# Counting graph edges on TensorE: ten chunks per PSUM bank, window offsets in registers, layer-norm sums by ScalarE

## The reference, cut to what matters

```python
x: (1250, 512) float32          # 1250 nodes
src, dst: (41250,) int32        # edges, both directions and one loop per node, sorted by dst
h = layernorm(x)                # mean and variance of each row of 512
for l in range(3):              # graph convolution
    h = relu(segment_sum((h @ W[l])[src] * norm, dst) + b[l])      # norm from the in-degrees
x = x + h                       # then: a small feed-forward part, a second graph layer,
                                # and a mixture of 16 experts with a shared one
```

## Time and profile before

| | us |
|---|---|
| median of 3 timed runs | 893.25 |
| lowest, highest | 893.14, 895.17 |
| the profiled execution's own time | 889.73 |
| its span in the profile | 887.7 |

### The profile page before, as it was taken

One profiled execution on the slowest core, in us unless ns is written; L12 is line 12 of the kernel. 1 busy time (PEld: TensorE's weight loads), 2 busy tenths in 40 slices (PEclk: granted clock), 3 DMA queues, 4 the chain that ended last, 5 costly groups with the idle time before them and its releaser, 6 DMA issues.

```text
span 887.7 us, 13725 instructions
## 1 busy us (share of the span) xinstructions
PE 807.3 (91%) x4032; PEld 624.7 (70%) x4033; DVE 554.3 (62%) x996; ACT 331.0 (37%) x624; POOL 141.9 (16%) x186
## 2 busy tenths in 40 slices
PE   4988799999999996998899987998989999999983
PEld 2444578888888875666788875787767777777761
DVE  7987491341242189789313479589557787778761
ACT  2567251341251111444221222332335556555541
POOL 2000000000000030000000330111313444455422
PEclk9999989999999998899999996996989999999997
DMA  7400000000000001000010302100989868965542
GB/s 189 136 1 1 2 1 0 1 1 1 1 1 1 6 25 49 1 1 1 0 48 1 113 1 66 50 1 1 327 287 365 223 170 288 326 195 82 127 92 35
DMA packets 32293, 71.39 MB, mean 80 GB/s; under 512 B 4387, under 2 KB 4637, under 8 KB 32243
## 3 DMA queue, kind: packets, MB, share of 16 engines
q1 hardware_dynamic: 24480, 53.31, 17.4%
q0 software_dynamic: 6272, 14.68, 8.3%
q10 hardware_dynamic: 1491, 2.73, 0.9%
HBM read 96.53 MB, written 12.72 MB: 123 GB/s over the span
## 4 chain that ended last, share of the span: by engine, by line
PE 72%; DVE 15%; issue 4%; ACT 3%; DMA 2%; ACTq 1%; DVEq 1%; POOL 0%; POOLq 0%
PE PS L1069 21%; PE PS L1103 9%; PE PS L1322 9%; PE PS L1369 8%; PE PS L1000 6%; PE PS L1201 5%; PE PS L1316 4%; PE PS L1144 3%; ACT CTR L717 2%; PE PS L1300 1%; DVE XN L1439 1%; PE PS L1331 1%; PE PS L1354 1%; PE PS L1043 1%; DVE stats L1846 1%
## 5 line engine op out<-in xcount | busy, mean ns | idle before, releaser
L1069 PE MATMUL PS<-CTR,YH 125*128 125x500 f32 (+1 forms) x480 | 164.1, 357 | 2.3 <-DVE YL L1620 2.3
L1069 PE MATMUL PS<-CTR,YL 125*128 125x500 f32 (+1 forms) x480 | 163.6, 356 | 0.0
L1069 PEld LDWEIGHTS PS<-CTR,YH 125*128 125x128 f32 x480 | 91.5, 191 | 15.6 <-DVE YL L1620 2.6
L1069 PEld LDWEIGHTS PS<-CTR,YL 125*128 125x128 f32 x480 | 91.6, 191 | 13.0
L1000 PE MATMUL PS<-ET 125*128 125x130 f16 x494 | 72.2, 303 | 16.0 <-ACT CTR L717 9.2
L1940 DVE TENSOR_TENSOR W1L<-WB,W1H 128x1152 fp32r<-128x1152 f32 x56 | 73.9, 1356 | 16.8 <-issue 8.4
L1369 PE MATMUL PS<-WB,YF 128*128 x168 | 76.9, 594 | 2.4 <-issue 1.7
L1647 DVE TENSOR_TENSOR ZL<-PS,ZH 128x500 fp32r<-128x500 f32 (+1 forms) x36 | 21.1, 591 | 90.1 <-ACT ZH L775 90.0
L1000 PEld LDWEIGHTS PS<-ET 125*128 125x128 f16 x494 | 39.9, 122 | 49.1 <-ACT CTR L717 28.7
L1322 PE MATMUL PS<-W1H,XGH 128*128 128x384 f32 x168 | 73.5, 438 | 0.0
L948 ACT CAST W1H<-WB 128x1152 fp32r x56 | 64.2, 1151 | 16.4 <-issue 10.3
(11 more groups left out here) (376 smaller groups left out, 1628.0 us busy)
## 6 DMA issues: line engine op xcount, KB each, us to landing
WB<-in_w SPq DMA_DIRECT2D x28, 1536.0 KB
WB<-in_w SPq DMA_DIRECT2D x28, 768.0 KB
WB<-in_b SPq DMA_DIRECT2D x28, 384.0 KB
X<-in_x SPq DMA_DIRECT2D x1, 2240.0 KB
xn_dram<-XN SPq DMA_DIRECT2D x1, 2240.0 KB
WNEXT<-in_W SPq DMA_DIRECT2D x2, 1024.0 KB, 9.5
SR<-in_sw SPq DMA_DIRECT2D x1, 1536.0 KB, 7.7
out<-X ACTq DMA_DIRECT2D x1, 1120.0 KB
```

The costliest lines, as they stand in the source:

```text
L1069: mm = nc.tensor.matmul(dest, lhs, rhs, start=(t == 0 and h == 0), stop=(t == NT - 1 and h == 1))
```

## The change

One PSUM bank now takes a whole batch (five pairs, ten chunks) with a window of 50 columns plus one (`BWIN`, 10 x 51 = 510 columns). A product has 12 columns for each of 10 tiles, and TensorE writes it at the pair's offset inside the bank's window. The offsets come from a table `off_i`, which VectorE computes once, and which TensorE reads into registers 25 at a time (five batches). Because the products only add, the bank is first set to zeros by a product of one row with a blank row of 510 columns (`open_bank`). It is issued for the next batch when the present one has two pairs left. `oh_next` is gone; one product of 10 columns for each batch (`first_column`) gives the last column of a window the edges that the next batch's first chunk still has for it, and it signals `group_done`, once a batch. ScalarE makes one copy of 10 x 50 columns for each batch.

Row sums of x (batches 2 to 11) and sums of squared deviations (batches 14 to 23) are taken by ScalarE with its accumulating output; VectorE then makes `XHAT` in ten operations after the last batch. The checks move into the batches (after batches 2 and 5), and TensorE waits for `counts_ready` only on the general way.

```diff
+PER = BATCH
+AHEAD_OF = 5
+CHECK_AT = 2
+FLAG_AT = 5
+SUMS_AT = 2
+SQUARES_AT = 14
+DEV_AT = 26
-WIN = 12
-SLOTS = WIN + 1
+SLOTS = 12
+BWIN = 50
+BKEYS = NT * (BWIN + 1)
+LAST_OFF = BWIN + 1 - SLOTS
...  ScalarE
+            for b in range(NBAT):
+                act.wait_ge(group_done, b + 1)
+                if b:
+                    act.wait_ge(placed, b)
+                nc.scalar.copy(CTR[0:NP, :, bass.ds(places[b % LOADS], BWIN)],
+                               PS[0:NP, b % 6, 0:BKEYS].rearrange("p (t w) -> p t w", t=NT)[:, :, 1:BWIN + 1]
                                ).then_inc(placed, 1)
+                t = b - SUMS_AT
+                if 0 <= t < NT:
...
+                    nc.scalar.activation(val[0:NP, t % 2, :], X[0:NP, t, :], ACT.Identity,
+                                         accum_out=sums[0:NP, 0, t:t + 1]).then_inc(sums_ready, 1)
+                t = b - SQUARES_AT
+                if 0 <= t < NT:
...
+                    nc.scalar.activation(val[0:NP, t % 2, :], X[0:NP, t, :], ACT.Square, bias=minus[0:NP, t:t + 1],
+                                         accum_out=sums[0:NP, 1, t:t + 1]).then_inc(sums_ready, 1)
...  TensorE
+            def first_column(b, past):
+                k = (b + 1) % RING
+                return nc.tensor.matmul(windows(b)[:, :, bass.ds(past, 1)], oh_lo[k][0:CHUNK, 0, :, 0],
+                                        oh_key[k][0:CHUNK, 0, :, 0].rearrange("p (t w) -> p t w", t=NT)[:, :, 0:1],
+                                        start=False, stop=True)
+
+            def open_bank(b):
+                if b >= 6:
+                    pe.wait_ge(placed, b - 5)
+                nc.tensor.matmul(PS[0:128, b % 6, 0:BKEYS], iota_lo[0:1, :, 0], blank[0:1, :], start=True, stop=False)
+
+            following = offsets(0)
+            open_bank(0)
+            for b in range(NBAT):
+                pe.wait_ge(onehot_ready, b + 1)
+                if b:
+                    first_column(b - 1, places[(b - 1) % AHEAD_OF * PER + PER - 1]).then_inc(group_done, 1)
+                if b % AHEAD_OF == 0:
+                    places = following
+                for j in range(PER):
+                    if j == PER - 2 and b + 1 < NBAT:
+                        open_bank(b + 1)
+                        if b % AHEAD_OF == AHEAD_OF - 1:
+                            following = offsets(b + 1)
+                    place = bass.ds(places[b % AHEAD_OF * PER + j - 1], SLOTS) if j else slice(0, SLOTS)
+                    for x in range(OWN):
+                        mm = nc.tensor.matmul(windows(b)[:, :, place], oh_lo[b % RING][0:CHUNK, j, :, x],
+                                              oh_key[b % RING][0:CHUNK, j, :, x].rearrange("p (t w) -> p t w", t=NT),
+                                              start=False, stop=(j == PER - 1 and x == OWN - 1 and b == NBAT - 1))
...
+            pe.wait_ge(placed, NBAT)
-            pe.wait_ge(counts_ready, 1)
...  VectorE
             for b in range(NBAT):
                 if b >= RING:
+                    dve.wait_ge(group_done, b - RING + 1)
                 onehots(b).then_inc(onehot_ready, 1)
+                if b == CHECK_AT:
+                    check_order()
+                    check_windows()
+                if b == FLAG_AT:
+                    set_flag()
+                if b == SQUARES_AT - 1:
+                    dve.wait_ge(sums_ready, NT)
+                    v.tensor_scalar(minus[0:NP, :], sums[0:NP, 0, :], -1.0 / D, None, ALU.mult).then_inc(mean_neg, 1)
+                if b == DEV_AT - 1:
+                    dve.wait_ge(sums_ready, 2 * NT)
+                    v.tensor_scalar(mv[0:NP, :, 1], sums[0:NP, 1, :], 1.0 / D, EPS, ALU.mult, ALU.add).then_inc(var_ready, 1)
+
+            dve.wait_ge(sd_ready, 1)
+            link(v.reciprocal(rstd[0:NP, :], sd[0:NP, :]))
+            for t in range(NT):
+                v.tensor_scalar(XHAT[0:NP, t, :], X[0:NP, t, :], minus[0:NP, t:t + 1], rstd[0:NP, t:t + 1],
+                                ALU.add, ALU.mult).then_inc(val_ready, 1)
```

More of the change, by code:

```diff
@@ L229, in build @@
         rstd = sb("rstd", [128, NT])
-        shift = sb("shift", [128, NT])
+        sums, minus = sb("sums", [128, 2, NT]), sb("minus", [128, NT])
         dis = sb("dis", [128, NT])
@@ L700, in _, with window_places @@
             act.wait_ge(windows_ready, 1)
-            def window_places(g):
-                row = wbase_i[0:1, g:g + LOADS]
+            def window_places(b):
+                row = place_i[0:1, b:b + LOADS]
                 return nc.values_load_multi_w_load_instructions(
-                    row, engines=(mybir.EngineType.Activation,), min_val=0, max_val=N,
-                    skip_runtime_bounds_check_because="DVE clamps the table to 0..N")[1]
+                    row, engines=(mybir.EngineType.Activation,), min_val=0, max_val=CW - BWIN,
+                    skip_runtime_bounds_check_because="DVE clamps the table to 0..CW - BWIN")[1]
@@ L995, in _ @@
             nc.tensor.matmul(PS[:, 7, 0:NCH], ones[0:1, :], dstf[0:1, 0:NCH], start=True, stop=True).then_inc(base_read, 1)
[L997 to L1015, removed]
@@ L1017, in _, with offsets @@
-            pe.wait_ge(bad_ready, 1)
-            nc.tensor.matmul(PS[:, 6, 0:1], ones[0:NP, :], bad[0:NP, 0:1], start=True, stop=True).then_inc(bad_sum, 1)
+            pe.wait_ge(const_done, 6)
+            pe.wait_ge(windows_ready, 1)
+            windows = lambda b: PS[0:128, b % 6, 0:BKEYS].rearrange("p (t w) -> p t w", t=NT)
+            def offsets(b):
+                clamped = "DVE clamps the table to the window"
+                cols = nc.values_load_multi_w_load_instructions(
+                    off_i[0:1, b * PER:(b + AHEAD_OF) * PER], engines=(mybir.EngineType.PE,), min_val=0,
+                    max_val=BWIN, skip_runtime_bounds_check_because=clamped)[1]
+                return [c if k % PER == PER - 1 else
+                        nc.s_assert_within(c, 0, LAST_OFF, skip_runtime_bounds_check_because=clamped)
+                        for k, c in enumerate(cols)]
@@ new lines, in _ @@
+            following = offsets(0)
[16 more added lines that the diff above has]
+                                              start=False, stop=(j == PER - 1 and x == OWN - 1 and b == NBAT - 1))
+                if b == FLAG_AT - 1:
+                    pe.wait_ge(bad_ready, 1)
+                    nc.tensor.matmul(PS[:, 6, 0:1], ones[0:NP, :], bad[0:NP, 0:1], start=True, stop=True
+                                     ).then_inc(bad_sum, 1)
@@ L1020, in group @@
+            mm.then_inc(group_done, 1)
             def group(lo_of, key_of):
@@ L1049, in _ @@
             with pe.If(slow > 0):
+                pe.wait_ge(counts_ready, 1)
                 degrees(ones[0:NP, :], CT)
@@ L1478, in _ @@
[L1478 to L1481 removed]
+            link(v.tensor_scalar(edge[0:1, :], wbase[0:1, 0:NG:PER], 1.0, 0.0, ALU.add, ALU.max))
```

153 lines of the change are left out of this document (61 added, 92 removed).

## The result

The changed kernel takes 886.16 us (median of four runs, 885.05 to 888.51), beside 893.19 us (893.04 to 895.17) for the kernel before. The ratio over all runs is 0.9915, with a 95% interval of 0.9891 to 0.9939. It is faster, as forecast, but by 7 us where 32 were expected, and the time lies outside the range.

The account below looks back on a forecast made before the run. ScalarE's copies clocked the counting stage; TensorE would pace it afterwards. Degrees 31.2 us earlier plus 1.0 for the clock took 889.73 to 857.5 us profiled; forecast on the median's scale 861.0, range 857 to 866.

Parts of the forecast that it names:

- The register loads: Counting stage, TensorE: seven loads of 25 registers, bounds 0 and 7 us, taken as 0.6 us with row-sum waits.
- TensorE's pace: Counting stage: ten products 1.00, zeros 0.425, first column 0.07; 1.50 us a batch, expected to set the pace.
- the last copy to the degrees: End of counting stage: TensorE passes `placed` and a branch, about 0.35 us, where 1.97 us was before.
- the clock term: Degree matmuls: if the clock is up by then they save 2.0 us; between 0 and 2.0, 1.0 taken.
- ScalarE left the path: Counting stage: ScalarE needs 42 us where 82 was, with passes taken at 0.75 us, so it leaves the path.
- VectorE's batch: Counting stage: one-hots `oh_lo` 0.74 and `oh_key` 0.70, together 1.44 us a batch, starting at 10.65.
- `XHAT` is hidden: End of counting stage: VectorE's ten operations, 4.7 us by busy time, are hidden; up to 1 us if cover were gone.
- The checks after batch 2: Counting stage, VectorE: order check 2.1 and window check 1.4, so 3.5 us on the path.
- rival A: Counting stage: the clock rises within it, VectorE's 1.44 us a batch becomes the pace; 857.7 us, chance 0.23.
- B: TensorE's sequencer: register instructions and loads not covered, about 2.0 us a batch; 13.5 us back, 874.5 us, chance 0.14.
- C: Counting stage: each register instruction waits until earlier products left the array; 3.05 us a batch, 912 us, chance 0.04.
- D: Counting stage: a window is overrun and the flag sends everything the general way, thousands of us; chance 0.01.

Follow-up runs that it names:

- the four-batch version: The changed kernel with AHEAD_OF 5 -> 4, so TensorE loads 20 offsets at a time in place of 25: 867.2 us, ratio 0.974 to the kernel before.
- the warmed version: AHEAD_OF 4 with one-row zeros, plus 24 extra float32 matmuls of 128 columns on TensorE before the first batch: 866.37 us.

## Why the prediction failed, by its own steps

**The register loads: the failed step.** The prediction bounded them at "7 x 1.0 = 7 us (25 registers at ScalarE's rate, uncovered)" and took 0.6 with the waits for the row sums. The loads alone left 20.0 us uncovered. The upper bound rested on a duration of another engine's load, of eight values, and took the price for one of count alone. It depends on the address too, and the trace of before held no such load on TensorE; on ScalarE the prediction read the delay of the next copy, not the load's own length. The shift of the table by four bytes shows the cause both ways. Had all loads been as short as the fifth, the 0.6 would have held at this clock: the four-batch version has 0.5 us of such idle.

The trace of before did hold the length of ScalarE's load, in a row that the prediction doesn't use (count: shortest/median/longest in ns):

```profile
L704 ACTq TENSOR_LOAD <-ET x21: 538/547/766, 9.6 to 92.8; - x21
```

Eight values take 0.55 us there, 0.07 us a value, the rate of TensorE's short loads. From it 25 values are an estimated 1.7 us (25 x 0.55 / 8), and the uncovered bound 7 x 1.7 = 12 us in place of 7. That would still have been 8 us short of the 20.0 measured: the long loads, at 0.24 us a value, have no row in that trace.

**TensorE's pace: mis-sized.** 1.50 us a batch was 10 x 0.100 + 0.425 + 0.07. The first and the last term were right (0.10 and 0.08), though for the last, 0.07, no row of the trace of before stood. The zeros cost 0.25 ahead and 0.53 behind, 0.26 more than the 0.10 + 0.425 in the sum. They come with the one-row operand: 125 rows give 1.53. Its weights, and those of the product behind it, are loaded only as the product starts, and with 125 rows ahead of it; moving the semaphore wait changed nothing. Why a load of one row isn't done ahead stays open.

These two make up the miss, 94.67 - 68.0 = 26.7 us at the degrees' start. Short loads take 19.8 of it away (94.67 to 74.84). Of the 6.8 left, 6.7 are the pace: from the start of batch 6 (26.72) to the end of the last product (73.97) it takes 47.2 us where 40.5 were forecast. The rest nearly cancels: batch 6 starts 0.9 us later than 25.8, the 0.6 for loads and waits isn't spent in this stretch, and the last copy to the degrees is 0.2 shorter.

With both undone the degrees start at 68.50, where 68.0 was forecast. Part of that agreement is luck: in that version the clock rises in places, which the forecast didn't assume, and its loads leave 6.9 us uncovered, most of it where the clock is up. Its 862.06 us is a profiled execution, whose counterpart in the prediction is 857.5, not 861.0. Of the 4.6 us between them some 3.2 lie behind the degrees' start (791.7 us in place of 788.5), 1.0 is the clock term that didn't come, and 0.5 the degrees' start.

**What held.** ScalarE left the path: passes of 0.63 and 0.72 us with 0.19 for reading the sum, 0.72 and 0.81 from the start of the one to the end of the other where 0.75 was taken, and 37 us spent waiting. VectorE's batch is 1.43 us (1.44), the one-hots start at 10.45 (10.65). The last copy to the degrees is 0.2 (0.35). `XHAT` is hidden. The checks after batch 2 cost VectorE 3.4 us (3.5), and the version with later checks shows that they were on the path. What follows the degrees' start took 788.5 us in both.

**The clock term** (1.0 us, from 0 to 2.0) came out as 0: 4.63 us from the degrees' start to the first copy of their sums in place of 4.64. The idle ahead of the degrees did shrink, to 0.9 us. In the four-batch version, with the same 0.9 us, it is 3.94 us (74.84 to 78.78); what moves the rise, these runs don't separate. In the version with 125 rows the clock is 1.00 from 60 to 68 us and 0.50 from 70 to 72, and the first copy comes after 4.19 us (68.50 to 72.69). So a clock that was up in the stage did not stay up for the degrees, though rival A counted on it.

**The rivals.** *B*, the sequencer not covered at 2.0 us a batch, was nearest in kind, and its 874.5 us was still too little: it spread the cost over all register instructions, while the products around the five address instructions of a batch keep their 0.10 us, and one load in five batches costs it all. *A*, the upper clock within the stage, didn't come. The Trainium skill, "TensorE: Matmul & The Clock Gate", section "What's actually happening", has sustained activity release the low rate; the warmed version has products in flight for all of ten microseconds at 0.50, so this trace doesn't agree. With 125 rows for the zeros it did come in part. *C* and *D* fell: products overlap throughout, and the window way was taken.

**The range.** It counted the load's unknown price at 7 us and cut it off at half of rival B. An instruction that this trace had never shown on this engine, in this size, stood seven times on the bounding engine; the price at which it would have eaten the whole gain (31 us / 7, or 4.5 us each) should have been set against what was known, and nothing shown excluded it.

## What to carry to other kernels

Let each load of many registers on TensorE start on a multiple of 16 bytes, or price it at 0.24 us a value instead of 0.07; a count that is a multiple of four 4-byte values keeps a table aligned that starts so, and 25 did not. Where the clock is up, expect most of even a short load to show. An operation that is cheap by its work (a product of one row) can cost its neighbours: look at the distance from the instruction before and to the one behind, not at its length. And if an instruction has no row in the trace of before, ask at what price it would undo the gain, and keep that price in the range until a row excludes it.

## What the runs showed of the hardware

- A load of registers on TensorE's sequencer takes 1.36 us for 20 values and 1.88 for 25 if it starts at a multiple of 16 bytes of the table (0.07 us a value), and 4.74 and 5.90 if not (0.24 us a value). The first of a kernel takes some 0.2 us more.
- At 1.2 GHz the short load of 1.88 us at 61.4 is hidden whole, and of the 5.9 us of the long ones 3.3 to 4.7 show, so 1.2 to 2.6 us are hidden. With 125-row zeros, where the clock is up in part, 5.1 to 5.6 of 5.9 us show, 1.6 of 1.88, and up to 1.1 of 1.36.
- A product of 510 columns with one row starts 0.25 us behind a product of 120 columns, and the next one 0.53 behind it; with 125 rows 0.10 and 0.43. Around the one-row product the weight loads start with their products, around the 125-row one 0.11 and 0.42 us ahead of them.
- With one-row products in it the stage stays at a granted 0.50 (1.2 GHz) even where products are in flight all the time; with 125 rows it reaches 1.00 (2.4 GHz) for stretches, and the batch takes 0.81 us there.
- In these traces the granted clock reads 1.00 ahead of its first fall, whatever it was: the spacing of the products (0.10 us for 120 columns) says 1.2 GHz in the changed kernel, and in the warmed version 11 and then 21 matmuls in two microseconds both read 1.00.
- ScalarE's accumulating output has a second instruction, of 0.19 us, behind each pass.
